# Weights from the twelfth unit on by chains of Prelu passes, with GpSimd taking the first right pass and the high half, and four rows of h to DRAM and back

## The reference, cut to what matters

```python
xn = _layernorm(x)
K = _s4_kernel(Lambda, p, q, B, Ct, step, 512)
y = irfft(rfft(xn, 1024) * rfft(K, 1024))[..., :512] + D * xn
w = NF4_CODE[q] * absmax_of_block          # Wg, Wu: 1792 x 512; Wd: 512 x 1792
h = silu(xn @ Wg.T) * (xn @ Wu.T)          # 2048 x 1792
out = x + y + h @ Wd.T
```

## Time and profile before

| | us |
|---|---|
| median of 3 runs (469.71 to 470.01) | 469.71 |
| profiled execution, its own time | 468.71 |
| its span, first to last instruction | 466.9 |
| PE busy in the span | 447.6 |
| DVE, ACT, POOL busy | 397.0, 276.3, 52.9 |

### The profile page before, as it was taken

The page is one execution under the profiler, slowest core; times in us unless marked ns, Lnnn a source line. Parts: engine busy times, 40 slices in busy tenths (PEclk is TensorE's granted clock), DMA queues, the critical chain, the costliest instruction groups (busy, mean ns, idle before and its releaser), DMA issues.

```text
span 466.9 us, 7151 instructions
## 1 busy us (share of the span) xinstructions
PE 447.6 (96%) x2607; PEld 254.5 (55%) x2607; DVE 397.0 (85%) x651; ACT 276.3 (59%) x463; POOL 52.9 (11%) x100
## 2 busy tenths in 40 slices
PE   0599999999999999999999999999999999999997
PEld 0454444444444444444544444466544688888886
DVE  4999689979797687888999558887899999999993
ACT  8866466587597665769768465884132543545340
POOL 0454499300000000000001000000000000000000
PEclk9999999999999999999999999999999999999999
DMA  8382554121223112213132315346400021101111
GB/s 284 83 286 71 111 94 140 47 86 51 71 65 91 50 42 76 61 45 92 51 107 70 92 22 147 97 136 228 161 0 0 2 91 46 41 6 47 46 46 45
DMA packets 30167, 38.81 MB, mean 83 GB/s; under 512 B 12917, under 2 KB 14005, under 8 KB 30133
## 3 DMA queue, kind: packets, MB, share of 16 engines
q1 hardware_dynamic: 30132, 38.37, 27.5%
HBM read 31.74 MB, written 4.52 MB: 78 GB/s over the span
## 4 chain that ended last, share of the span: by engine, by line
PE 91%; issue 3%; DVE 3%; POOL 2%; ACT 1%; POOLq 0%
PE bank L1818 38%; PE bank L2054 21%; PE bank L1949 17%; PE bank L2007 8%; PE bank L1997 6%; POOL h L658 1%; PE bank L1853 1%; DVE h L1098 0%; DVE h L1261 0%; PE bank L1908 0%; DVE bank L1205 0%; DVE work L1092 0%; DVE work L1088 0%; DVE work L1074 0%; ACT work L752 0%
## 5 line engine op out<-in xcount | busy, mean ns | idle before, releaser
L1818 PE MATMUL bank<-xT,w 128*128 128x512 f16 (+1 forms) x828 | 183.2, 376 | 3.4 <-DVE w L1098 1.9
L1818 PEld LDWEIGHTS bank<-xT,w 128*128 128x128 f16 x828 | 80.6, 98 | 98.5 <-DVE w L1098 2.1
L752 ACT ACTIVATE work<-work 128x512 f32<-128x512 int32 x152 | 86.5, 621 | 3.5 <-DVE work L1074 2.3
L2054 PE MATMUL bank<-wd,work 128*128 128x256 f16 x504 | 56.2, 273 | 0.0
L2054 PEld LDWEIGHTS bank<-wd,work 128*128 128x128 f16 (+1 forms) x504 | 49.3, 98 | 6.0
L1034 ACT ACTIVATE work<-h 128x896 f16<-128x896 f32 x30 | 28.0, 943 | 28.6 <-DVE h L1726 21.6
L818 ACT ACTIVATE work<-bank,sc 128x512 f32<-128x512 f32 x47 | 31.8, 678 | 19.4 <-PE bank L1818 19.1
L2054 PE MATMUL bank<-h,work 128*128 128x256 f16 x378 | 42.2, 273 | 0.0
L2054 PEld LDWEIGHTS bank<-h,work 128*128 128x128 f16 x378 | 37.0, 98 | 4.3
L1949 PE MATMUL bank<-h 128*128 128x512 f16 x150 | 36.5, 379 | 0.0
L2007 PE MATMUL bank<-wd,h 128*128 128x512 f16 x168 | 36.4, 379 | 0.0
(11 more groups left out here) (194 smaller groups left out, 583.1 us busy)
## 6 DMA issues: line engine op xcount, KB each, us to landing
h<-in_x SPq DMA_DIRECT2D x8, 512.0 KB, 4.6
xT<-in_x SPq DMA_DIRECT2D x16, 256.0 KB, 4.4
out<-xT SPq DMA_DIRECT2D x15, 256.0 KB, 2.0
work<-in_q_gate SPq DMA_DIRECT2D x14, 256.0 KB, 2.6
work<-in_q_up SPq DMA_DIRECT2D x14, 256.0 KB, 2.7
work<-in_am_gate SPq DMA_DIRECT2D x28, 128.0 KB, 3.0
work<-in_am_up SPq DMA_DIRECT2D x28, 128.0 KB, 2.9
work<-in_q_down SPq DMA_DIRECT2D x14, 256.0 KB, 2.8
```

The source lines that it names most:

```text
L752: nc.scalar.activation(knee_of(u, k), qs[:, u % 2, :], KNEE, scale=scale, bias=bias, alpha=below).then_inc(knee_done, 1)
L1818: mm = nc.tensor.matmul(out_b, weights(k)[:, unit, wl, f, :], xT[:, TPC * c + first:TPC * c + last, xl, f, :], start=(i == 0), stop=(i == ...
L2054: mm = nc.tensor.matmul(out_b, part, w, start=(n == 0), stop=(n == 3 * KT - 1))
```

## The change

It does five things. All windows from k = 3 to 13 become blocked; so that rows 10 to 13 stay scratch, tiles 10 to 13 of h are written into rows 0 to 3, after what stood there has been stored to DRAM (`h_out`), and comes back into rows 10 to 13 before the down products (`h_back`). Units from the 12th on (`CHAINED`, u = 11 to 41) are made by two chains of three Prelu passes each, left and right, one in the output of the other, so that DVE has only WHOLE, SCALED and `weight_lo` left. POOL makes the first right pass of each (`first_pass`) and the high half of u = 11 to 37 (`weight_hi`). The whole weights rotate through three rooms. POOL also issues the loads of the residual. One down unit more is made early (`EARLY_IN` has a 6), and `toeplitz(2)`, `(3)`, `(4)` move to later slots.

```diff
-BLOCKED = range(3, 12)
+BLOCKED = range(3, NM)
-EARLY_IN = (5, 9, 10, 11, 12)
+EARLY_IN = (5, 6, 9, 10, 11, 12)
+CHAIN_ORDER = ("l0", "r0", "l1", "r1", "l2", "r2")
-LAST_UNITS = 4
+LAST_UNITS = 3
+CHAINED = range(11, UNITS)
+POOL_HALVES = range(CHAINED[0], UNITS - 4)
+MOVED = 4
+HOME = [mt if mt < NM - MOVED else mt - (NM - MOVED) for mt in range(NM)]
...
+        def chain_room(u, side):
+            return knee[:, u % 2 + (2 if side == "r" else 0), :]
+        def room_read(u):
+            return dq_after(u - 1, LEFT) if u == CHAINED[0] else dq_after(u - 2, WHOLE)
         def whole_of(u):
+            if u in CHAINED:
+                return acc[:, (u - CHAINED[0]) % 3, :]
...
+            def h_out(mt):
+                sp.wait_ge(h_done, max(len(OPENING), NCH * (mt + 1)))
+                sp.wait_ge(hlo_done, SPLIT * max(3, mt + 1))
+                sp.dma_start(moved[:, mt, :], h_f32[:, mt, :]).then_inc(moved_st, 16)
+            def h_back(c):
+                if c == 0:
+                    sp.wait_ge(m_done, len(BLOCKS) * len(BLOCKED))
+                    sp.wait_ge(moved_st, 16 * MOVED)
+                part = slice(CH * c, CH * (c + 1))
+                sp.dma_start(h_f32[:, NM - MOVED:NM, part], moved[:, :, part]).then_inc(moved_ld[c], 16)
...
+                for mt in range(MOVED):
+                    if place == made_before(5 + mt):
+                        h_out(mt)
...
-            load_residual(0, 2)
...
-            load_residual(8, NT)
+            sp.wait_ge(xr_ld[NT - 1], 16)
+            for c in range(NCH):
+                h_back(c)
...
+            pool.wait_ge(v_done, V_STEPS)
+            first_pass(CHAINED[0])
+            for u in POOL_HALVES:
+                first_pass(u + 1)
+                weight_hi(u)
+                if u == made_before(NM - 3) - 1:
+                    turned_rows()
+                if u == made_before(NM - 2) + 1:
+                    kernel_max()
+            first_pass(UNITS - 3)
+            first_pass(UNITS - 2)
+            for t in range(NT):
+                pool.wait_ge(conv_done, t + 1)
+                pool.dma_start(res[:, t, :], x_v[:, t, :]).then_inc(xr_ld[t], 16)
+                if t == 3:
+                    first_pass(UNITS - 1)
...
             def toeplitz_stage(slot):
-                if 4 <= slot < 7:
-                    toeplitz(slot - 2)
+                if slot >= 6:
+                    toeplitz(slot - 4)
...
             for mt in range(NM):
-                pe.wait_ge(wlo_done, PLACE[GU + mt] + 1)
+                pe.wait_ge(wlo_done, PLACE[GU + DOWN_ROWS.index(mt)] + 1)
+                if mt == NM - MOVED:
+                    pe.wait_ge(moved_ld[0], 16)
```

More of the change, by code:

```diff
@@ L503, in codes_of @@
                 u = SEQ[place]
-                load_codes(place, q_down[u - GU] if u >= GU else (q_gate, q_up)[u % 2][u // 2])
+                load_codes(place, q_down[TILE[DOWN_ROWS[u - GU]]] if u >= GU else (q_gate, q_up)[u % 2][u // 2])
             def absmax_of(place):
                 u = SEQ[place]
[L508 to L514, removed]
+                load_absmax(place, am_down[TILE[DOWN_ROWS[u - GU]]] if u >= GU else (am_gate, am_up)[u % 2][u // 2])
             def turn(t):
@@ L736, in _, with turned_rows @@
-            pool.partition_all_reduce(kmax, krow, P, bass.bass_isa.ReduceOp.max).then_inc(kmax_done, 1)
+            def turned_rows():
+                pool.wait_ge(u_done, 4)
+                for c in range(2):
+                    for a in range(4):
+                        if a == 0:
+                            row = turns[:, 0, c:c + 1].to_broadcast([P, 4])
+                        else:
+                            row = turns[:, a, c:c + 3 * a + 1:a]
+                        pool.tensor_copy(turned[:, c, a, :], row).then_inc(turn_done, 1)
@@ new lines, in weight_hi @@
+            def weight_hi(u):
+                pool.wait_ge(dq_done, dq_after(u, SCALED))
+                unit = SEQ[u]
+                if unit < GU:
+                    before = room_before(unit // 2)
+                    if unit % 2 and before in BLOCKED:
+                        pool.wait_ge(m_done, m_at(before, 4))
+                    else:
+                        pool.wait_ge((gate_done, up_done)[unit % 2], WHOLE_COUNT[LAST_USE[before]])
+                pool.tensor_scalar(weight_of(u)[HI], whole_of(u), scale_of(u), None, ALU.mult).then_inc(phi_done, 1)
@@ L848, in block_hi @@
                 w_sums = sums_room(k)[1]
-                first, last = sums_parts(k)[part]
+                first, last = SUMS_PARTS[part]
                 nc.scalar.activation(sums_split(k, first, last)[:, :, HI].rearrange("p i f m -> p i (f m)"),
@@ L957, in _ @@
             silu(9)
[L958 removed]
+            items(ACT_AT[7], ACT_AT[7] + 3)
             token_hi(0)
@@ L1100, in items @@
             def items(first, last):
-                for p in range(first, min(last, DVE_ITEMS * UNITS)):
-                    u, i = p // DVE_ITEMS, p % DVE_ITEMS
+                for p in range(first, last):
+                    u, i = item_of(DVE_AT, p)
+                    if u in CHAINED:
+                        i = (3, 2, 4)[i]
                     if i != 2:
@@ L1498, in window @@
-                for c in range(NCH):
-                    n = NCH * k + c
+                n = NCH * k
+                if k == NM - MOVED:
+                    dve.wait_ge(moved_st, 16 * MOVED)
+                if k == BLOCKED[0]:
                     h_mul(n)
-                    items(at + per * 2 * c // 8, at + per * (2 * c + 1) // 8)
-                    if stage:
-                        stage(2 * c)
                     h_lo(n)
-                    items(at + per * (2 * c + 1) // 8, at + per * (2 * c + 2) // 8)
-                    if stage:
-                        stage(2 * c + 1)
+                    stage_of(0, 2)
+                    join(k, 0)
+                    stage_of(2, 4)
+                else:
+                    stage_of(0, 2)
+                    h_mul(n)
+                    stage_of(2, 3)
+                    h_lo(n)
+                    stage_of(3, 4)
+                    join(k, 0)
@@ L1509, in _ @@
+                stage_of(4, 6)
+                join(k, 1)
+                h_mul(n + 3)
+                stage_of(6, 7)
+                h_mul(n + 1)
+                stage_of(7, 8)
+                block_of(other_sums, k + 1)
+                block_of(block_lo, k + 1, 0)
+                h_mul(n + 2)
+                block_of(block_lo, k + 1, 1)
             for k in range(3, NM - 7):
```

273 lines of the change are left out of this document (134 added, 139 removed).

## The result

The changed kernel takes **483.45 us** (median of 4 runs, 482.45 to 485.58), the kernel before 469.78 us in the same session: ratio 1.0296, 95% interval 1.0256 to 1.0336, so 3% slower. The forecast was 482.0 us within 473.5 to 488.5. The profiled execution took 482.45 us, with a span of 480.5.

A forecast was written before the change was run, and what follows sets the result against it. PE's gapless matmul chain was taken as the bound: 466.9 - 2.6 + 1.6 + 11.8 + 1.5 = 479.2 us span, plus 1.8 and 1.0 to a median of 482.0 us, range 473.5 to 488.5.

The forecast's parts named there:

- The removal, -2.6: Two windows of 96 matmuls become two of 90: 12 x 0.216 = 2.6 us less.
- Windows of k = 12 and 13, +11.8: POOL's maximum with a switch on each side delays `first_pass(35)` and `block_lo`; PE waits 11.8 us at m5 of k = 13.
- The R of 7.5: Assumed cost in us of one POOL switch, a gap beside the maximum; bounds 4.8 and 9.5.
- Window of k = 11, +1.6: `first_pass(30)` behind POOL's copies makes the join late; PE waits 1.6 us at m3, bounds 0 and 2.5.
- Restart, +1.5: After a wait of 12 us PE may run at half pace for a few us: 1.5, bounds 0 and 2.1.
- h rows, residual loads, convolution and down products, 0: Row stores and their return, POOL's issue of the residual, and the last products cost 0; convolution and down products up to 1.
- POOL's passes as such, 0: POOL's 31 first passes and 27 high halves cost PE 0, up to 1 us if somewhere a join slips.
- The median: Taken 1.0 us above the profiled execution, as in the kernel before, giving 482.0 from 481.0.
- The switch is cheap: Rival on POOL's maximum: nothing slips, median 467.1, chance 0.09; or the k = 11 join waits, 468.8, chance 0.07.
- POOL's DMA issue is the slow one: Rival: POOL needs 2.5 us to issue each residual load, weight sums begin 13 us late, 495 us; chance 0.05.
- POOL and DVE slow each other in every window: Rival: DVE loses more than the 4.1 us it sheds per three-unit window; some 5 us more, chance 0.02.

The follow-up runs named there:

- experiment 7: Changed kernel with the maximum by two small DMAs on GpSimd's queue, turned rows behind first_pass(30), first passes of units 11 and 12 released earlier: 468.44 us, ratio 0.9979.
- Experiment 1: Changed kernel with GpSimd copying each partition's own value in place of the maximum over 128 partitions: 472.6 us, ratio 1.0060.
- experiment 8: Experiment 1's kernel with three pairs of maximum and `tensor_scalar` added at the end of GpSimd's queue: 472.76 us, ratio 1.0066.
- Experiment 3: Changed kernel with the eight small copies of the turned rows moved behind first_pass(30), ahead of weight_hi(29): 481.67 us, ratio 1.0259.
- experiments 9 and 10: Each on Experiment 1's kernel: stores of the h rows made twice, 471.96 us; the sixteen residual loads issued by SP, not GpSimd, 471.84 us.
- Experiment 4: Changed kernel with first right passes of units 11 and 12 waiting for DVE's RIGHT step of unit 10, not its LEFT and WHOLE: 483.7 us, ratio 1.0292.
- experiment 6: Experiment 1's kernel plus SP storing the 128 row maxima to DRAM, for whose landing nobody waits: 479.11 us, ratio 1.0185.
- experiment 5: Changed kernel with the edits of Experiment 3 and Experiment 4 and the maximum by DMA on SP's queue, its waits behind due codes: 475.96 us, ratio 1.0136.

## Why the prediction was right, and where it was off

**The removal, -2.6: right.** 2595 matmuls for 2607, PE still gapless between its waits, and with the new waits taken away (experiment 7) the kernel ends under the one before.

**Windows of k = 12 and 13, +11.8: right in where PE waits and in what ends the wait, measured 10.0.** Term by term from 268.58: the high half ended at +14.9 (15.6 predicted), the switches took 6.43 and 7.03 (7.5 each), the maximum 0.38 (0.7), the first pass 1.97 (0.8), and the rest to `block_lo`'s end 5.2 (5.6); PE wanted it at +26.1 (25.9). The R of 7.5 was my estimate from the 9.5 us ahead of `ident`; no run shows that those 9.5 us were a switch, and R was 0.5 to 1.1 too high each. Ahead of the maximum of the kernel before no switch is to be seen, only 30.9 us of wait for DVE, and nothing stood behind it that could show the second. Over the runs a switch measured 6.10 to 6.43 us to the maximum and 6.94 to 7.27 back, 10.34 once. Besides, a first pass, which reads int32, cost 1.2 more than an idle `norm`. ACT's wait inside the chain, forecast at some 16 us, was 11.12: its pass before had itself waited 2.94 for codes, to 287.58. Experiment 1 shows that the switches are the cause, experiment 8 that they cost only because of where they stand.

**Window of k = 11, +1.6: right, measured 1.86.** Three terms were off and nearly cancelled: DVE's step that releases the copies ended 6.4 us into the window (251.56 less 245.18, where it starts) for 5.7, eight copies took 1.04 for 2.07, the first pass 2.32 for 1.43. Experiment 3 removes the wait by order alone.

**Restart, +1.5: right, measured 1.65**, now with its granted clock beside it (0.50 to 0.57).

**h rows, residual loads, convolution and down products, 0: right.** No wait of PE there; experiments 9 and 10. The convolution and the two parts of the down products take 26.08, 36.26 and 96.30 us, to the hundredth what they took before.

**POOL's passes as such, 0: off by 1.2.** At k = 4 the join did not slip, but the first chained unit did: its first pass was released by DVE's LEFT step although it writes a room whose last reader is the RIGHT step, and the second unit's pass then lay beside DVE's sums. The bound of up to 1 us, "if somewhere a join slips", had been named; the place had not. Experiment 4 takes 0.67 of it. The price of a first pass was also too low: the 31 take 64.6 us in this trace, 2.09 each, where 1.43 or 0.76 was taken.

**The opening, not in the sum: 1.2 us.** GpSimd's chain of small operations, with the same instructions as before, hands over to `norm` later:

```profile
26.09 4.34 POOL L731 TENSOR_SCALAR h<-h 128x512 f32<-128x512 f32 x4
```

In the earlier trace rows it starts at 24.38. It is also shorter (4.34 for 5.73), but PE needs its parts one by one and gets to the transposes behind them at 28.98 for 27.71. PE's own matmuls just ahead ran at half pace in this trace (12 of 256 columns in 2.74 us for 1.48, at a printed granted clock of 1.00), but that does not set the time: in experiment 3, where they took 1.48, the same transposes started at 29.00, after a wait of 1.04 for `norm`. Two operations of GpSimd's chain take 1.20 and 1.41 us, in every run of the new program alike. Why is open; no experiment was made on it.

**The median** stood 1.0 above the profiled execution in the kernel before; here it was again 1.0 (483.45 for 482.45). Nothing in the working explains that: the profiled execution was the fastest of four, two of which lie at 482.5 and two at 484.4 and 485.6.

**The closeness of the sum is in part luck.** The forecast span was 479.2 for 480.5 measured. The term of k = 13 was 1.8 us too high, and the opening and k = 4, 1.2 us each, were not in the sum.

**Rivals.** *The switch is cheap*: out, in both its forms. *POOL's DMA issue is the slow one*: the issue took 0.54 us a load, not 2.5. *POOL and DVE slow each other in every window*: PE has no wait of 0.2 us or more in the windows of k = 5 to 10.

## What to carry to other kernels

The maximum over the partitions on GpSimd (`partition_all_reduce`, between `tensor_scalar` operations; no other kind was tried) came with two gaps in its queue in all four runs that have it among other work, the changed kernel and experiments 3, 4 and 8: 6.10 to 6.43 us ahead of it and 6.94 to 7.27 ahead of the next `tensor_scalar`, in one case 10.34. While GpSimd has nothing else to do both are free (experiment 8: 43.4 us of gaps, 472.76 us for 472.6); once it is given work that others wait for, look first for such a maximum that stands between its pieces, and move it out or replace it (experiment 1: 10.9 us less). A replacement by DMA must be judged by its queue as well: the store of 128 single values ahead of codes in SP's queue cost 6.5 us (experiment 6), and on GpSimd's queue, with codes(36) issued ahead of it, the kernel took 468.44 us for 475.96 (experiments 7 and 5).

## What the hardware showed unexpectedly

- A store of 128 single values (0.5 KB) landed 7.8 us after its issue, and a 256 KB load issued 0.43 us behind it in the same queue landed after 11 us, for 2.7 otherwise. Issued by GpSimd the same store took 9.2 us to land, and loads that SP issued meanwhile 5.0 and 6.0, which nobody noticed. What in the store is slow is open.
- A switch was 6.10 to 6.43 us towards the maximum and 6.94 to 7.27 back, and 10.34 while 4 MB were moving at a DMA share of 1.00 to 0.72. The 9.5 us ahead of `ident` at the start of the kernel before were no measure of it, 9.5 for 6.4 and 7.0: in the new program the same operation waited 0.36 us. Why it waited 9.5 in the one and 0.36 in the other, no run shows.
- The runs of one kernel lie on steps of the mean granted clock. In experiment 4: 481.5 and 481.9 us at 0.989, 483.6 to 484.2 at 0.986, 485.4 at 0.982. In experiment 7, where PE waits for 0.5 us at most behind the opening, nine of twelve runs are at 1.000 and within 1.1 us; in experiment 3, with its wait of 9.85, none is above 0.989. The long wait of the changed kernel cost its length, 10.0 us, and 1.65 us of half-pace restart. That it also widens the spread is not shown: experiment 1, without it, has one of six runs at 1.000 and lies 2.3 us apart, experiment 3 with it 2.1. The step can also come in the opening, as in experiment 1's profile (stretch, its length, busy us and count of PE, PEld, DVE, ACT, POOL, granted clock, DMA share, GB/s):

```profile
20.00:30.00 10.00, 8.21 (x46) 4.98 (x44) 9.68 (x18) 6.23 (x11) 9.14 (x14) 0.95 0.69 215
30.00:40.00 10.00, 10.00 (x46) 4.76 (x45) 6.47 (x18) 6.16 (x14) 0.77 (x1) 0.88 0.47 154
```
